# Indirect stores of ranked rows: one at the start of every step instead of two at the start of every odd step

## The reference

```python
q, k, v = heads(Wq @ ln(x) + bq), heads(Wk @ c + bk), heads(Wv @ c + bv)   # per batch, 8 heads, 256 positions
q, k = rotary(q), rotary(k)
p = softmax(q @ k.T / sqrt(8)); x = x + Wo @ (p @ v) + bo
xt = ln(x).reshape(4096, 256)
probs = softmax(xt @ Wr.T + bias); topk_val, topk_idx = top_k(probs, 2)
w = topk_val / (sum(topk_val) + 1e-9)
y_e = (silu(xt @ Wg[e]) * (xt @ Wu[e])) @ Wd[e]
out = x + sum_k w_k * y_{topk_idx_k} + silu(xt @ sWg) * (xt @ sWu) @ sWd
```

## Time and profile before

| what | value |
| --- | --- |
| median of 3 executions | 749.5 us (748.78 to 751.17) |
| the profiled execution, its own time | 750.0 us |
| span of its instructions | 748.1 us |
| PE busy | 703.8 us (94%) |
| DVE busy | 600.2 us (80%) |
| ACT busy | 467.4 us (62%) |
| POOL busy | 419.6 us (56%) |
| indirect stores L636 | 64, 63.8 us busy on POOL |
| PE's share of the chain that ended last | 81% |

### The profile page before, as it was taken

How to read it: one execution, slowest core, us unless ns; L and a number is a source line. 1 busy time by engine, 2 the same in 40 slices (tenths; PEclk the granted TensorE clock), 3 DMA queues, 4 the chain that set the end, 5 groups by cost and what they waited for, 6 DMA issues and landing times.

```text
span 748.1 us, 19315 instructions
## 1 busy us (share of the span) xinstructions
PE 703.8 (94%) x6067; PEld 508.1 (68%) x6067; DVE 600.2 (80%) x1580; ACT 467.4 (62%) x1086; POOL 419.6 (56%) x742
## 2 busy tenths in 40 slices
PE   3599999999999999999999999999989889999994
PEld 2366676666667676676666676676558878888883
DVE  6978888899899899989989998998747535466666
ACT  4056777776777777777777777777752255555441
POOL 5544645446657667656756657664345026565663
PEclk9999999999999999999999999999999999999998
DMA  9577444444554555554555455555166335678775
GB/s 285 142 191 205 126 129 120 134 124 122 142 143 131 140 142 147 150 143 131 139 151 148 137 145 134 145 138 144 55 220 200 108 87 170 209 248 276 252 229 167
DMA packets 98514, 118.76 MB, mean 159 GB/s; under 512 B 14317, under 2 KB 82672, under 8 KB 98417
## 3 DMA queue, kind: packets, MB, share of 16 engines
q1 hardware_dynamic: 90400, 99.53, 48.1%
q0 software_dynamic: 6864, 16.93, 6.5%
q10 hardware_dynamic: 1152, 1.07, 0.5%
HBM read 76.80 MB, written 42.11 MB: 159 GB/s over the span
## 4 chain that ended last, share of the span: by engine, by line
PE 81%; DVE 8%; issue 4%; POOL 3%; DMA 2%; ACT 1%; ACTq 1%; DVEq 0%; POOLq 0%; SPq 0%
PE bank_s L1271 15%; PE bank_o L1254 15%; PE bank_st L1299 14%; PE bank_st L1420 8%; PE bank_b L1286 7%; PE bank_s L1438 4%; PE bank_st L1232 3%; DVE M L1049 3%; PE bank_b L1313 2%; PE bank_b L1306 2%; PE bank_a L1354 2%; DVE st L854 2%; PE bank_a L1334 2%; PE bank_b L1345 2%; POOL results L700 1%
## 5 line engine op out<-in xcount | busy, mean ns | idle before, releaser
L1049 DVE TENSOR_REDUCE M<-bank_s 128x2 f32<-128x512 f32 x512 | 339.8, 683 | 41.0 <-PE bank_s L1271 38.4
L737 ACT ACTIVATE Pr<-bank_st 128x512 f32<-128x512 f32 x512 | 297.4, 598 | 117.2 <-PE bank_st L1299 104.6
L1271 PE MATMUL bank_s<-QK 72*128 72x256 bf16 x1024 | 200.6, 279 | 10.7 <-DMA QK<-parts 6.9
L1299 PE MATMUL bank_st<-QK 98*128 98x256 bf16 x1024 | 197.4, 274 | 2.4 <-DMA QK<-Mt 1.0
L666 POOL TENSOR_TENSOR work<-work 128x256 f32<-128x256 f32 x64 | 46.7, 730 | 170.1 <-DVE work L1083 170.1
L1254 PE MATMUL bank_o<-Pr,wide 128*32 128x256 f32 x2048 | 138.0, 385 | 0.0
L1271 PEld LDWEIGHTS bank_s<-QK 72*128 72x128 bf16 x1024 | 92.5, 99 | 66.3 <-DVE M L1049 34.9
L700 POOL DMA_INDIRECT results<-Pr,ids_out x79 | 78.5, 994 | 82.2 <-issue 41.5
L1299 PEld LDWEIGHTS bank_st<-QK 98*128 98x128 bf16 x1024 | 91.5, 98 | 38.9 <-ACT Pr L737 11.1
L1420 PE MATMUL bank_st<-QK,xn 128*128 x316 | 82.0, 382 | 0.6 <-issue 0.4
L1254 PEld LDWEIGHTS bank_o<-Pr,wide 128*32 128x32 f32 x2048 | 55.7, 109 | 34.5 <-issue 13.7
(11 more groups left out here) (151 smaller groups left out, 1033.3 us busy)
## 6 DMA issues: line engine op xcount, KB each, us to landing
QK<-parts SPq DMA_DIRECT2D x128, 288.0 KB
parts<-parts_sb SPq DMA_DIRECT2D x128, 96.0 KB, 2.3
wide<-slots SPq DMA_DIRECT2D x79, 130.0 KB, 2.4
ctx_kv<-ctx_dram SPq DMA_DIRECT2D x64, 128.0 KB, 2.4
xT_all<-results SPq DMA_DIRECT2D x14, 512.0 KB, 5.1
X<-x_dram SPq DMA_DIRECT2D x8, 512.0 KB, 6.9
parts<-parts_sb SPq DMA_DIRECT2D x64, 64.0 KB, 2.1
QK<-w_gu SPq DMA_DIRECT2D x8, 512.0 KB, 8.7
```

The source lines that it names most:

```text
L737: nc.scalar.activation(Pr[k][:], bank_st[k % 2][:], ACT.Exp, scale=SCALE).then_inc(s_exp, 1)
L1049: nc.vector.tensor_reduce(M[:, c, 2 * ORDER[k]:2 * ORDER[k] + 2], bank_s[S_BANK[c][k]][:].rearrange("p (a s) -> p a s", a=2), AX.X, ALU.ma ...
L1271: last = nc.tensor.matmul(bank_s[S_BANK[at.mod(2)][k]][:, T * t:T * t + T], Q[c][0:KR, ORDER[k], P * t:P * t + P], K[c][0:KR, ORDER[k], :] ...
L1299: last = nc.tensor.matmul(bank_st[k % 2][:, T * s:T * s + T], K[c][0:MROW + 2, ORDER[k], P * s:P * s + P], Q[c][0:MROW + 2, ORDER[k], :], ...
```

## The change

For the first five groups, `STORES` had two stores in each odd step from 19 to 57. Now it has one store in each step from 19 to 58. The order of the stores and the places of `number` stay; the second and fourth store of each set of four come one step later. The steps from 59 on are as before.

```diff
         STORES = {}
         for g in range(5):
             for k in range(2):
-                STORES[8 * g + 19 + 4 * k] = [("number", g, k, 0, 0), ("store", g, k, 4 * g, 4 * g + 2)]
-                STORES[8 * g + 21 + 4 * k] = [("store", g, k, 4 * g + 2, 4 * g + 4)]
+                for n in range(GROUP):
+                    STORES[8 * g + 19 + 4 * k + n] = [("store", g, k, 4 * g + n, 4 * g + n + 1)]
+                STORES[8 * g + 19 + 4 * k].insert(0, ("number", g, k, 0, 0))
```

## The result

The changed kernel took 755.85 us in the median of seven executions (752.39 to 757.81), the kernel before 749.5 (748.75 to 751.17, seven too): a ratio of 1.0079, interval 1.0058 to 1.0101. It is slower, and slower than the forecast of 751.4 and its range. The profiled execution of the changed kernel is the shortest of its seven, 752.39 us with a span of 750.6, so its trace shows less than half of the difference. The mean granted clock of TensorE is 0.998 and 0.995 in the two shortest of the seven (752.39 and 753.38) and 0.982 to 0.988 in the five others (755.04 to 757.81).

What follows compares the result with a forecast made beforehand. PE, busy 94% of the span, was taken to bound the kernel. Terms +1.0, +0.5, +0.7 and -0.3 made +1.9 us on the profiled 750.0, 751.9, lowered to 751.4 for the median; range 749.0 to 755.0.

Steps and rivals of the forecast that it cites:

- the hold: Even steps: SP's wait for the added store sends L516 1.72 us later, delaying parts writes and the next L507 1.6 us.
- The slack: Odd steps' L507: 6.0 us from issue to PE's need instead of 7.6; ten steps tight, nine with 0.8 more.
- The wait of 0.30 us, -0.3: PE's one wait at 282.45 for a DMA held by stores; one store fewer gives back at most 0.3 us.
- Step 59, +0.5 (0 to 1.3): Short step 59: L507 issued at 516.2 instead of 514.84, need 5.1 us later; costs 0 to 1.3, taken as +0.5.
- The ten tight steps, +1.0: Ten odd steps between 21 and 55: late L507 costs 0 to 0.4 us each, taken as 0.1, together +1.0.
- the slow landings of parts, +0.7: Late parts writes at two places seen (29 and 45), 1.2 to 1.7 us stall each; 0 to 3.4, taken as +0.7.
- No change: Rival, chance 0.25: L507 always lands within 5.1 to 6 us, parts never slow at a bad place; 749.2 us.
- Much later: Rival, chance 0.15: even-step store data lengthen the parts writes' 2.1 us by 0.4; 757.2 us at most, 754 in the middle.
- Faster: Rival, chance 0.06: two odd-step stores cause 8.49 us even steps; halving gives 0.22 us in each of five; 748.1 us.
- step 14: Sign against the faster case: before any store is issued, this step already lasts 8.49 us with PE busy 8.07.
- The rule of the Trainium skill: DMA takes about 2.0 us plus bytes at 436 GB/s: L507 lands in 3.3 us, no step tight, sum -0.3.

Runs made afterwards that it cites:

- f3_even_free: The changed kernel, but SP's queue isn't held for `s_stored` in the even steps 20 to 58; 749.51 us, ratio 1.0006 to before.
- f4_hold_alone: The kernel before with its stores, plus an idle POOL memset and SP's hold in even steps 20 to 58; 755.28 us, ratio 1.0091.
- g4_loose_only: The changed kernel, with even-step holds of SP only in the nine steps ahead of odd steps not called tight; 750.31 us, ratio 1.0004.
- f1_before: The kernel before, unchanged, run again beside the changed one for its trace; 750.36 us, ratio 1.0007.
- f2_after: The changed kernel, unchanged, run again for another trace; 756.77 us, ratio 1.0077 to before.
- g1_58_free: The changed kernel without SP's hold in step 58; 752.71 us, ratio 1.0038 to before.
- i1_58_fill: The changed kernel with step 58's hold alone of the even steps' holds, plus 12 thrown-away matmuls in step 60; 750.72 us, ratio 1.0016.
- i2_58_only: The changed kernel with step 58's hold alone of the even steps' holds, without filler matmuls, in a later set; 754.64 us, ratio 1.0057.
- g2_58_only: The changed kernel with step 58's hold alone of the even steps' holds; 752.41 us, ratio 1.0039 to before.
- h2_before_fill: The kernel before with 12 extra matmuls in step 60, in a set where before took 785.0 us; 785.31 us, ratio 1.0006.

## Why the prediction was wrong

**That the hold is what costs, and through which chain: right.** L517 of even steps came 1.72 us later (1.7 predicted), L508 of step 21 at 211.83 (211.8 predicted), PE's waits are ended by "DMA QK<-parts", L667 never waits for stores, and `f3_even_free` and `f4_hold_alone` show no other cost. The slack was read rightly in the main: `g4_loose_only` is at 1.0004, though step 27, counted among those with 0.8 us to spare, is late in two traces (7.87 us in that of after, 8.16 in that of `g4_loose_only`).

**The wait of 0.30 us, -0.3: there was nothing to give back.** Step 29 takes 7.52 us in the trace of after, where it took 7.81, but step 30 takes 8.49 where it took 8.21. The kernel before has the same lengths in the trace of `f1_before`, without the change; its steps 29 and 30:

```profile
274.16:281.68 7.52, 7.52 (x77) 5.18 (x75) 7.34 (x19) 5.40 (x13) 4.86 (x10) 1.00 0.50 143
281.68:290.18 8.50, 8.08 (x84) 5.74 (x81) 8.23 (x20) 6.43 (x14) 5.68 (x12) 1.00 0.53 141
```

So a wait of 0.3 us in an odd step was made up in the even step behind it, where PE has idle time to lose (8.50 us with PE busy 8.08), and it came and went without the change.

**Step 59, +0.5 (0 to 1.3): mis-sized.** It measured 1.85 us in the trace of after (8.53 for the 6.68 that it took before) and 1.70 in that of `f2_after`. The issue was foreseen (1.36 us after the step's start, measured 1.40), the landing was not: 7.0 us where 6.4 was the upper bound and 5 to 6 what I took. With the need 5.1 us behind the issue, every bit of a longer landing counts in full there. L508 lies beside two stores of step 59 itself; whether they lengthen it wasn't tried. It isn't the hold that lengthens it: in `g4_loose_only`, with no hold in step 58, PE waited for it until 6.9 us after the issue (515.39 to 522.25).

**The ten tight steps, +1.0, and the slow landings of parts, +0.7: mis-sized, and of another shape.** Together 1.7 was predicted, 1.4 with the -0.3. Steps 19 to 58 lost 1.64 us in the trace of after, which is the shortest of its seven executions, and 3.7 in that of `f2_after`. The loss isn't 0.1 in each of ten steps: it stands mainly in steps 23, 39 and 45, at up to 1.71 us of idle time, wherever a write of parts lands late on the new schedule. I had seen two such places and valued them at chance; each of the four traces has such places. By time this half is 3.1 us (`g1_58_free`, 752.71 against 749.63).

**What the sum left out: the clock.** Each term counted a wait at its own length, and TensorE's clock stood at nothing. Behind step 59's wait the granted clock was halved in three of the four traces with the whole change or the one hold, among those of the sets at 749 us, and steps 60 to 62 took 1.6, 2.8 and 4.7 us more there. `i1_58_fill` against `i2_58_only` shows 3.9 us of the median for that one wait. The rows ahead of the change showed 1.00 in every step, and I took it as given, though what they showed was a PE with hardly any idle time.

**How they add up.** The median of 755.85 lies 4.45 us above the forecast. In the trace of `f2_after`, 6.9 us longer than that of before by its own time, steps 19 to 58 give 3.7 (predicted 1.4), step 59 gives 1.7 (predicted 0.5) and the clock behind it 1.6 (predicted nothing): 5.1 us of miss in these three terms. All of them failed, and the first the most in that trace. By the medians, the holds ahead of step 58 cost 3.1 us where 1.4 was predicted, and the hold of step 58 costs 2.8 (`g2_58_only`) to 5.0 (`i2_58_only`), wait and clock together, where 0.5 was. What makes a write of parts land late in some executions and not in others, and what decides whether the clock falls, stays open.

**The rivals.** "No change" fell. "Much later" came nearest in time (754 to 757.2), but for another reason than the one it gave: the last writes of parts, which L508 waits for, still land in 2.1 us in the median, as in step 20 (209.71 to the issue of L508 at 211.83). Only the larger writes ahead of them (L526, now L527) went from 2.3 to 2.8. "Faster" was dismissed by step 14, rightly for the runs at 749 us, and not for those at 782: there, steps with two stores are up to 1.5 us longer (in the trace of `h2_before_fill`), and no row of the kernel before could have shown it. The rule of the Trainium skill that the prediction weighed (page "DMA: Bandwidth & Descriptors", section "Anatomy of one DMA — SWDGE (gpsimd) path") gave an estimated 3.3 us for L507. That section fits DMAs issued from GpSimd, and L507 is issued on SP's queue. It doesn't hold here: PE waited for the transfer until 7.0 us after its issue in step 59.

## What to carry to other kernels

When a wait is put on a DMA queue, cost what is issued behind it: here a 1.3 us store on POOL became a lateness of the next step's large load, nearly hidden ahead of nine steps and not ahead of ten others, and worst in the one short step. The loss lay in the few places where a write landed late, so cost the slow landings and not the median one. Where PE is nearly always busy, don't count a new idle time at its own length alone: waits of 1.5 to 1.7 us at the start of step 60 were followed by half clock in three of four traces, and 12 useless matmuls in its place gave back 3.9 us. And take the trace of an execution near the median: that of the result was the shortest of seven, and its clock never fell in this stage. The better edit is to take away the wait of the even steps (`f3_even_free`, 1.0006), or to leave the stores where they were; where it takes 749.5 us no version beat the kernel before.

## What was not expected of the hardware

- The same kernel has two times, each steady within a set: 749.5 to 749.7 us in four sets, 782.4 and 785.0 in two. The granted clock doesn't tell them apart (0.987 in the profiled execution of `h2_before_fill`, 0.983 in that of `g2_58_only`). In the trace of `h2_before_fill` ACT sees PE's product late while stores are being issued, and in both longer sets the kernels with one store for two are 1.7 to 2.5% faster. Sets of either kind stand beside the same chip number, so I can't say what makes the difference. Why the product is seen late stays open.
- The transfer of 576 KB by L508 was awaited for 6.8 to 7.0 us in step 59, in five traces, against 4.9 to 6.4 in the earlier trace rows.
- Adding 12 matmuls made a kernel 3.9 us faster. In the two traces the clock was halved behind the wait without them, and stayed at the upper level with them.
